# Moving the next pair's input normalisation within the cross-attention phase of a transformer sandwich kernel

## The reference

```
y  = layernorm(x)
a1 = causal self attention (16 heads of 8) of layernorm(y)*g1+b1, projected, + y
a2 = cross attention of layernorm(a1)*gx+bx to 256 encoder tokens, projected, + a1
m  = gelu MLP (128 -> 512 -> 128) of layernorm(a2)*g2+b2, + a2
x' = x + layernorm(m)
z  = layernorm(x')                  # the input of the mixture of experts
x''= x' + layernorm(shared expert + top-2 of 8 routed SwiGLU experts)
```

## Time and profile before

| | us |
|---|---|
| median of three runs | 1620.1 |
| the profiled execution | 1619.62 |
| its span in the trace | 1617.8 |
| TensorE matmuls busy | 1428.0 (88%) |
| VectorE busy | 1114.0 (69%) |
| ScalarE busy | 986.8 (61%) |
| GpSimd busy | 317.5 (20%) |

### The profile page before, as it was taken

One profiled execution on the slowest core, in us unless ns is written; L12 is line 12 of the kernel. 1 busy time (PEld: TensorE's weight loads), 2 busy tenths in 40 slices (PEclk: granted clock), 3 DMA queues, 4 the chain that ended last, 5 costly groups with the idle time before them and its releaser, 6 DMA issues. The chain is left out here.

```text
span 1617.8 us, 39137 instructions
## 1 busy us (share of the span) xinstructions
PE 1428.0 (88%) x15448; PEld 876.0 (54%) x15448; DVE 1114.0 (69%) x3252; ACT 986.8 (61%) x1618; POOL 317.5 (20%) x428
## 2 busy tenths in 40 slices
PE   2677799989899999989899999989999998989887
PEld 1445565655556465655656565565646565555442
DVE  5656676777777677777777677677767767646344
ACT  2255676675857576675757577585757666572642
POOL 3420221121213121121213121121312112020120
PEclk7678899999999999999999999999999999997898
DMA  3324111213040312213040221304031211010000
GB/s 70 58 75 57 48 29 41 36 34 49 14 69 10 54 29 38 39 25 58 10 74 10 46 30 38 45 18 65 10 60 24 38 32 36 2 29 8 15 7 7
DMA packets 79214, 58.05 MB, mean 36 GB/s; under 512 B 11004, under 2 KB 78902, under 8 KB 79030
## 3 DMA queue, kind: packets, MB, share of 16 engines
q1 hardware_dynamic: 76726, 53.90, 19.0%
q10 hardware_dynamic: 2304, 1.64, 0.7%
HBM read 11.57 MB, written 4.19 MB: 10 GB/s over the span
## 5 line engine op out<-in xcount | busy, mean ns | idle before, releaser
L1035 DVE TENSOR_REDUCE chunkmax<-ps 128x3 f32<-128x384 f32 (+1 forms) x1024 | 506.8, 554 | 105.9 <-PE ps L1389 100.3
L711 ACT ACTIVATE probs<-ps 128x768 f32<-128x768 f32 (+1 forms) x512 | 408.1, 808 | 172.6 <-PE ps L1384 167.4
L1454 PE MATMUL ps<-zT,w 128*128 128x512 f32 x576 | 281.0, 602 | 6.5 <-ACT silu_a L728 4.8
L728 ACT ACTIVATE silu_a<-ps,b 128x512 f32<-128x512 f32 x144 | 98.7, 685 | 197.7 <-PE ps L1454 174.4
L1369 PE MATMUL ps<-k_op,q_op 48*128 48x256 bf16 x512 | 144.8, 286 | 51.6 <-DVE chunkmax L1035 37.6
L1176 DVE SCALAR_TENSOR_TENSOR h_open<-ps,b,silu_a 128x512 f32<-128x512 f32 x128 | 95.8, 749 | 123.4 <-PE ps L1454 111.1
L1454 PEld LDWEIGHTS ps<-zT,w 128*128 128x128 f32 x576 | 102.8, 191 | 114.6 <-issue 87.4
L1351 PE MATMUL ps<-q_op,k_op 51*128 51x256 bf16 x512 | 142.4, 278 | 17.1 <-POOL lower L499 9.3
L1490 PE MATMUL ps<-hT,w 128*128 128x512 f32 x288 | 149.3, 599 | 3.8 <-DVE hT L1182 3.0
L1369 PE MATMUL ps<-xk_op,xq_op 51*128 51x256 bf16 x512 | 144.6, 284 | 5.1 <-DVE chunkmax L1035 4.5
L1381 PE MATMUL ps<-xmask_q_lo,ident_lo 64*128 64x262 bf16 x512 | 144.1, 283 | 0.0
(11 more groups left out here) (245 smaller groups left out, 3435.8 us busy)
## 6 DMA issues: line engine op xcount, KB each, us to landing
q_op<-q_parts SPq DMA_DIRECT2D x192, 64.0 KB
xq_op<-xq_parts SPq DMA_DIRECT2D x192, 64.0 KB
k_op<-k_parts SPq DMA_DIRECT2D x168, 64.0 KB
x_tm<-in_L_attn_hidden_states SPq DMA_DIRECT2D x16, 256.0 KB, 5.9
x_keep<-in_L_attn_hidden_states SPq DMA_DIRECT2D x16, 256.0 KB, 6.2
out<-o_tm SPq DMA_DIRECT2D x16, 256.0 KB, 2.3
k_op<-k_parts ACTq DMA_DIRECT2D x24, 64.0 KB
w<-in_L_ffn_rw SPq DMA_DIRECT2D x1, 1024.0 KB
```

What stands on the lines that cost most here:

```text
L711: act.activation(probs[:, four % 2, 2 * pair:2 * pair + 2, 0:T + a.seen], ps[:, 2 * (1 - g % 2):2 * (1 - g % 2) + 2, 0:T + a.seen], ACT.Ex ...
L1035: dve.tensor_reduce(chunkmax[:, b, at, :], ps[:, MAX_BANK[n], 0:3 * a.seen].rearrange("p (c n) -> p c n", c=3), AX.X, ALU.max).then_inc(a. ...
L1454: pe.matmul(ps[:, bank, :], w, src[:], start=True, stop=True).then_inc(sig.sem, 1)
```

## The change

`norm_x` gets a first and a last block, and is called twice: blocks 0 and 1 behind E6, blocks 2 and 3 behind E10. The call behind E14 goes. Each call has its own two waits (`sa.xT_ps` and `sa.nb`). No other instruction is added, removed or moved on any engine. Line numbers behind line 812 rise by 2.

```diff
-            def norm_x(j):
+            def norm_x(j, first=0, last=NB):
 
                 act.wait_ge(*sa.xT_ps.before(j))
-                normalise(sa, x1_tm, x_tm, (tiny[:, 5, :], tiny[:, 9, :]), sa.x_ready, j)
+                normalise(sa, x1_tm, x_tm, (tiny[:, 5, :], tiny[:, 9, :]), sa.x_ready, j, first, last)
...
                 if exists(i - 1):
-                    exps(ca, i - 1, used, 4, 8)
+                    exps(ca, i - 1, used, 4, 6)
+                if exists(i + 2):
+                    norm_x(i + 2, 0, 2)
+                if exists(i - 1):
+                    exps(ca, i - 1, used, 6, 8)
...
                 if exists(i - 1):
-                    exps(ca, i - 1, used, 8, 11)
-                if exists(i - 1):
-                    exps(ca, i - 1, used, 11, 12)
+                    exps(ca, i - 1, used, 8, 10)
+                if exists(i + 2):
+                    norm_x(i + 2, 2, NB)
+                if exists(i - 1):
+                    exps(ca, i - 1, used, 10, 12)
...
                 if exists(i - 1):
-                    exps(ca, i - 1, used, 12, 14)
-                if exists(i + 2):
-                    norm_x(i + 2)
-                if exists(i - 1):
-                    exps(ca, i - 1, used, 14, H)
+                    exps(ca, i - 1, used, 12, H)
```

## The result

The changed kernel takes 1606.89 us (median of four runs, 1605.14 to 1607.44) against 1620.97 us before on the same chip (four runs, 1617.73 to 1624.36). The ratio is 0.9918, 95% interval 0.9899 to 0.9936: faster by 0.8%, 14.1 us between the medians. The forecast was 1607.0, with a range of 1603 to 1612.5.

The account below looks back on a forecast made before the run. TensorE was taken as the bound (matmuls busy 88%), losing time in the cross phase. 12 x 1.05 + 0.54 = 13.1 us off 1619.62 gives 1606.5, plus 0.5 for the median: 1607.0 us, range 1603 to 1612.5.

Parts of the forecast that it names:

- The cost of the group: End of the cross phase: the x1_tm copies on ScalarE delay TensorE's last value group by 1.05 us, in 12 phases.
- i = 1: First cross phase with the group: no z_tm copies, ScalarE less late, so the gain is only 0.54 us.
- The pieces in the idle time: ScalarE behind E6 and E10: each 0.77 us piece fits the 0.80 us idle time, 0.14 us left, cost 0.
- a second cover: Behind piece one: 0.28 us idle before E10 and TensorE's 0.81 us wait for VectorE would absorb an overrun.
- The 0.23 us before score group 15: TensorE's idle time there: read as waiting for E13 behind z_tm, making the scores of E15 late; expected to stay.
- The chain behind V8: From the last value group onward: everything starts earlier with it, nothing absorbs the gain, whole 13.1 us kept.
- The sum: Total gain over i = 1 to 13: 12 x 1.05 + 0.54 = 13.1 us.
- rival D: Cross phase end: all 1.44 us idle before the last value group and 0.23 us go, 1599.2 us; chance 0.03.
- rival C: TensorE's clock dips shift in steady phases: 0.4 us less to 5.3 more, 1606.6 to 1612.3; chance 0.06 beyond forecast's range.
- A: Piece behind E10 does not fit: up to 9.2 us given back, 1616.2 us, with half 1611.6; chance 0.10.
- B: Both pieces land on TensorE's path: 20.0 us price against 13.1 gained, slower at 1627.0 us; chance 0.02.
- E: Later in the iteration something not following TensorE absorbs the gain: 1620 us; chance 0.07.

Follow-up runs that it names:

- E6: Not a run: exponential pair on ScalarE in the cross phase; piece one of the change stands behind it.
- E10: Not a run: exponential pair on ScalarE in the cross phase; piece two of the change stands behind it.
- E14: Not a run: exponential pair on ScalarE late in the cross phase; the x1_tm group stood behind it before the change.
- e3: Changed kernel with blocks 2 and 3 put back behind E14, blocks 0 and 1 still behind E6: 1607.52 us, ratio 0.993 to the kernel before.
- E11: Not a run: exponential pair on ScalarE in the cross phase, the next behind piece two.
- E13: Not a run: exponential pair on ScalarE in the cross phase, the next behind the z_tm copies.
- E7: Not a run: exponential pair on ScalarE in the cross phase, the next behind piece one; score group 9 needs it.
- e1: Changed kernel with all four x1_tm blocks behind E6, none behind E10: 1606.03 us, ratio 0.9923 to the kernel before.
- e2: Changed kernel with all four x1_tm blocks behind E10, none behind E6: 1614.58 us, ratio 0.9964 to the kernel before.
- E15: Not a run: exponential pair on ScalarE late in the cross phase; it followed the x1_tm group before the change.
- e5: Changed kernel with the z_tm copies also split, blocks 0 and 1 ahead of E13, 2 and 3 behind E14: 1605.3 us, ratio 0.9911.
- e4: Changed kernel with all four x1_tm blocks moved behind the last exponential pair, both other calls gone: 1609.1 us, ratio 0.9938 to the kernel before.
- e8: The changed kernel unaltered, measured again beside the kernel before on the same chip: 1604.72 us, ratio 0.9906.
- e6: Changed kernel with norm_x in cross phases writing only 8 of 128 features per block: 1605.99 us, ratio 0.9915 to the kernel before.

## Why the prediction was right, point by point

**The cost of the group, from the phase without it.** Right. 1.05 us a phase was worked out from i = 14, and the iteration fell by 1.07 (92.00 to 90.93). The half move of e3 shows the threshold behind that number: a group's cost is what reaches past the arrival of the scores behind it, not its length.

**i = 1.** Right: V8 is 176.58 - 175.60 = 0.98 us behind V7, 0.54 less than before. E11 came late as said, and ScalarE's idle time ahead of E13 took it: 0.50 us there instead of 0.80.

**The pieces in the idle time.** Right for both, to 0.01 us (E11) and 0.00 (E7): they start as far behind E10 and E6 as they did when they waited for their scores. That piece one had a second cover and piece two had none was argued from the order of waits; e1 and e2 show it, with 0.01 and 0.57 us an iteration for the same lateness.

**The 0.23 us before score group 15.** Wrong. I took it for a wait for E13 behind z_tm, and gave it as the reason why E15's scores come late. e5 took that cause away: 0.20 us stay, without a releaser, as ahead of the other score groups behind a value group in which TensorE waits for nobody. E15's scores come when TensorE has made them. The number did not enter the sum, but rival D counted it in, and its price was too high by that.

**The chain behind V8.** Right: the whole gain of a phase is found in the iteration. e4 measures one link of it: zT later by 0.30 us made the iteration longer by 0.32.

**The sum.** 13.1 us forecast, 14.1 between the medians beside the first result, 14.9 on the chip of e8, 12.1 between the two spans. The steady part is 12 x 1.07 = 12.8 and i = 1 0.54, 13.4 together. The difference of -1.3 to 1.5 us is not larger than what the ends differ by in two profiles of the changed kernel (e8); rival C had looked for the clock in the steady phases only. Whether a shorter iteration also helps or harms at the ends was not shown. That the forecast of 1607.0 us meets 1606.89 to 0.1 us is luck: the base that it was worked out from, 1620.1, was 0.9 us below the later median of the kernel before, and the gain was a microsecond larger than forecast.

**Rivals.** A falls by e6, B by e1 (nothing was exposed behind E6) and by the changed profile, C in the steady phases by the profiles (one dip before, one now, none in e8), while outside them single stretches moved by 1 to 2 us; D fails on V8's 0.40 us, which stayed, and E by the iteration. On C the prediction read only one of the longer iterations before. Three more of them (i = 5, 7 and 12: 92.28, 92.28 and 92.30 us) were longer at a granted clock of 1.00, so not every longer iteration is a dip; the changed profile has as much of this, and it cancels. Nor do the short waits ahead of the dip explain it: TensorE's waits of 0.61 and 0.29 us for VectorE stand in front of the dip of i = 10, but the changed profile has the same pair in the phase of i = 8, where the clock stays at 1.00.

## What to carry to other kernels

Look for a pass of the same loop that by its index lacks the instruction in question: it prices the instruction, with everything hidden behind it, before any experiment. Side work belongs where the consumer of the next main step is itself waiting for something else, and how late a step may be is asked of its reader, not of the gap in front of it: the same 0.64 us were free behind E6 and cost 0.57 behind E10. Where like instructions have the same gap in front of them without a releaser (here 0.20 us), only what goes beyond it is a wait (here 0.03), even if a releaser's name stands on the whole.

## What the runs showed that I had not expected

The ends of the span vary more than the middle. In two profiles of the changed kernel eleven steady iterations together differ by 0.37 us, and the spans by 3.5. Over the profiles of all versions i = 1 to 2 took from 71.64 to 75.70 us and i = 15 to 16 from 81.22 to 82.80; for the kernels before and after, the granted clock was 0.72 against 0.86 and 0.64 against 0.58 in the windows shown. In a kernel with such ends, a difference under 2 us is read from the period of the steady part.
